# Local attention on one core: projections as three float32r products of high and low parts in place of one fp32 product

## What is computed

```python
def local_attn(x, Wqkv, Wout):          # x is the layer norm with scale ln_w and shift ln_b
    qkv = x @ Wqkv.T                    # (b, 512, 128) @ (128, 1536)
    q, k, v = jnp.split(qkv, 3, axis=-1)
    q, k, v = map(towin, (q, k, v))     # 8 windows of 64 rows, 8 heads of 64
    ke, ve = (expand(k), expand(v))     # each window with its two neighbours
    sim = jnp.einsum('bhnid,bhnjd->bhnij', q, ke) * SCALE
    attn = jax.nn.softmax(jnp.where(valid, sim, -1e9), axis=-1)
    o = jnp.einsum('bhnij,bhnjd->bhnid', attn, ve)
    return o @ Wout.T
```

## Time and profile before

| | |
|---|---|
| median of 3 runs | 1968.98 us (1967.86 to 1974.41) |
| profiled execution, span | 1969.3 us |
| TensorE products busy | 1812.7 us, 92% |
| TensorE weight loads busy | 1293.1 us, 66% |
| VectorE busy | 1463.0 us, 74% |
| ScalarE busy | 1463.6 us, 74% |
| GpSimd busy | 548.0 us, 28% |
| granted TensorE clock, mean | 0.973 |
| projections to queries and keys (L817), each light stage, in pj alone | x244, 132.4 us |
| projections to values (L820), first and second light stage | x128, 69.2 us; x122, 66.4 us |

### The profile page before, as it was taken

The page is one execution under the profiler, slowest core; times in us unless marked ns, Lnnn a source line. Parts: engine busy times, 40 slices in busy tenths (PEclk is TensorE's granted clock), DMA queues, the critical chain, the costliest instruction groups (busy, mean ns, idle before and its releaser), DMA issues. The chain is left out here.

```text
span 1969.3 us, 67306 instructions
## 1 busy us (share of the span) xinstructions
PE 1812.7 (92%) x27305; PEld 1293.1 (66%) x27305; DVE 1463.0 (74%) x3594; ACT 1463.6 (74%) x4168; POOL 548.0 (28%) x668
## 2 busy tenths in 40 slices
PE   3889889888999999999979978899999999997998
PEld 1444444444677777777768865567777777776886
DVE  8999999995676777778865656656777777786553
ACT  4999999984888888887735547588888888773553
POOL 1000000001344444444431107334444444443110
PEclk7999999998999999999989979999999999998998
DMA  6555555530000000000010000010101010002001
GB/s 196 145 141 141 156 142 142 142 77 12 13 19 19 18 19 19 19 23 15 24 46 1 2 1 1 1 23 13 24 13 24 14 24 15 23 19 51 28 28 33
DMA packets 77917, 91.88 MB, mean 47 GB/s; under 512 B 11485, under 2 KB 67650, under 8 KB 77090
## 3 DMA queue, kind: packets, MB, share of 16 engines
q1 hardware_dynamic: 76314, 87.15, 17.5%
q10 hardware_dynamic: 1296, 0.44, 0.1%
HBM read 39.67 MB, written 31.10 MB: 36 GB/s over the span
## 5 line engine op out<-in xcount | busy, mean ns | idle before, releaser
L1419 POOL TENSOR_TENSOR f1l_pn<-f1l_p,f1l_rs 128x512 f32<-128x512 f32 (+1 forms) x256 | 207.9, 833 | 326.0 <-DVE f1l_rs L1140 325.1
L1419 POOL TENSOR_TENSOR f2l_pn<-f2l_p,f2l_rs 128x512 f32<-128x512 f32 (+1 forms) x256 | 207.9, 834 | 297.5 <-DVE f2l_rs L1140 297.4
L1021 ACT ACTIVATE f2l_p<-f2l_sm,f2l_nb 128x192 f32<-128x192 f32 x512 | 212.0, 434 | 44.4 <-DVE f2l_nb L1133 44.4
L1021 ACT ACTIVATE f1l_p<-f1l_sm,f1l_nb 128x192 f32<-128x192 f32 x512 | 211.8, 432 | 42.4 <-DVE f1l_nb L1133 42.4
L513 ACT ACTIVATE r_pr<-r_far 128x1536 f32<-128x1536 f32 x128 | 195.4, 1527 | 3.4 <-PE r_far L387 3.1
L403 PE MATMUL r_acc<-r_pr,r_vp 128*32 128x128 f32 (+2 forms) x3584 | 191.4, 330 | 5.0 <-DVE r_pr L616 3.7
L608 DVE SCALAR_TENSOR_TENSOR r_pr<-r_pr,k_lo,r_cap 128x512 f32<-128x512 f32 x256 | 179.7, 743 | 7.0 <-ACT r_pr L513 6.8
L616 DVE TENSOR_SCALAR r_pr<-r_pr,k_hi,k_lo 128x768 f32<-128x768 f32 x256 | 161.7, 674 | 0.0
L513 ACT ACTIVATE r_pr<-r_near 128x1024 f32<-128x1024 f32 x128 | 139.7, 1091 | 1.5 <-PE r_near L374 1.4
L817 PE MATMUL f1l_pj<-f1l_xt,k_wqkv 128*128 128x512 f32 x244 | 132.4, 624 | 2.6 <-ACT f1l_kt L1003 1.4
L817 PE MATMUL f2l_pj<-f2l_xt,k_wqkv 128*128 128x512 f32 x244 | 132.4, 624 | 2.2 <-ACT f2l_kt L1003 1.4
(11 more groups left out here) (440 smaller groups left out, 4876.8 us busy)
## 6 DMA issues: line engine op xcount, KB each, us to landing
rbf_rows<-r_part SPq DMA_DIRECT2D x112, 128.0 KB, 2.2
r_qs<-rbf_rows SPq DMA_DIRECT2D x60, 192.0 KB
r_ks<-rbf_rows SPq DMA_DIRECT2D x60, 192.0 KB
f1l_vs<-f1l_vv SPq DMA_DIRECT2D x64, 128.0 KB, 2.4
f2l_vs<-f2l_vv SPq DMA_DIRECT2D x64, 128.0 KB, 2.4
rbf_rows<-r_part SPq DMA_DIRECT2D x16, 384.0 KB, 3.0
rbf_rows<-r_part SPq DMA_DIRECT2D x16, 256.0 KB, 3.1
out<-k_x SPq DMA_DIRECT2D x16, 256.0 KB, 2.3
```

The costliest lines, as they stand in the source:

```text
L1021: ins = nc.scalar.activation(p[:, u % 2, k, :], sm[:, u % 2, k // 2, k % 2 * PW:(k % 2 + 1) * PW], ACT.Exp, bias=nb[:, u % 2, k:k + 1], ac ...
L1419: ins = nc.gpsimd.tensor_tensor(pn[:, u % 2, at:at + HU * w].rearrange("p (k c) -> p k c", k=HU), p[:, u % 2, :, cols], r.broadcast_to([P, ...
```

## The change

Both operands of the projections are kept as two float32r parts: high is the value rounded to float32r, low is the rest, rounded in turn. One projection is three products that add up in one bank: low weights by high rows, high by high, high weights by low rows (for values the other way round).

- Weights: wqkv is no longer one load. In the first stage SyncE loads it in thirds to the tile `whole` after batches 1, 2 and 3, and GpSimd writes `wqkv_h` and `wqkv_l`, one copy and one subtraction for each third.
- Rows: xt becomes `xh` and `xl`, two buffers each. GpSimd makes them (`split`, a copy and a subtraction over 128 x 512), for batch 0 VectorE does (`split_first`).
- The transposes of z are no longer k = 0 of `use` but `turn_x`, with semaphores of their own (s_xp, s_xe), and stand at i = TURN_AT = NT - 2 = 2 in the lists of TensorE, ScalarE and GpSimd. They wait for s_pt of unit 2t + 1, the copy of tp by VectorE. In VectorE's list `late` is unchanged (`t % NT == NT - 1`).
- Memory: tiles of the first stage alone are freed after it, yt shares memory with qt, and `one` is a single column that is broadcast.

The core of the diff (new line numbers where a reader needs them are those of the rows of order below):

```diff
@@ stage_rbf, SyncE
             for b in range(B):
                 batch(b, b % 2)
+                if 0 <= b - SPLIT_AT < 3:
+                    q = b - SPLIT_AT
+                    wait(sp, s_wh, 2 * q)
+                    sp.dma_start(whole[:], A["wqkv"][:, THIRD * q:THIRD * (q + 1)]).then_inc(s_wl, 16)
@@ stage_rbf, GpSimd
+            for q in range(3):
+                w = slice(THIRD * q, THIRD * (q + 1))
+                pool.wait_ge(s_wl, 16 * (q + 1))
+                nc.gpsimd.tensor_copy(K["wqkv_h"][:, w], whole[:]).then_inc(s_wh, 1)
+                pool.wait_ge(s_wh, 2 * q + 1)
+                nc.gpsimd.tensor_tensor(K["wqkv_l"][:, w], whole[:], K["wqkv_h"][:, w], ALU.subtract).then_inc(s_wh, 1)
@@ stage_light
-        USES = 1 + 2 * HP + NT
+        USES = 2 * HP + NT
+        TURN_AT = NT - 2
@@ TensorE
-                    mm = nc.tensor.matmul(at, K["wqkv"][:, c * P:(c + 1) * P], xt[:], start=True, stop=True)
+                    w = slice(c * P, (c + 1) * P)
+                    nc.tensor.matmul(at, w_l[:, w], xh[:, par, :], start=True, stop=False)
+                    nc.tensor.matmul(at, w_h[:, w], xh[:, par, :], start=False, stop=False)
+                    if k == 1:
+                        pe.wait_ge(s_xs, 2 * b + 2)
+                    mm = nc.tensor.matmul(at, w_h[:, w], xl[:, par, :], start=False, stop=True)
...
-                    mm = nc.tensor.matmul(at, xt[:, j * P:(j + 1) * P], K["wqkv"][:, 2 * H * DH:3 * H * DH],
-                                          start=True, stop=True)
+                    rows, w = slice(j * P, (j + 1) * P), slice(2 * H * DH, 3 * H * DH)
+                    nc.tensor.matmul(at, xl[:, par, rows], w_h[:, w], start=True, stop=False)
+                    nc.tensor.matmul(at, xh[:, par, rows], w_l[:, w], start=False, stop=False)
+                    mm = nc.tensor.matmul(at, xh[:, par, rows], w_h[:, w], start=False, stop=True)
+
+            def turn_x(b):
+                if b == 1:
+                    pe.wait_ge(s_pe, 2 * HP + (0 if C else 1))
+                elif b > 1:
+                    pe.wait_ge(s_pt, UNITS * (b - 2) + 2 * TURN_AT + 2)
+                pe.wait_ge(s_z, b + 1)
+                at = bank(b, 0)
+                for j in range(NT):
+                    mm = nc.tensor.transpose(at[:, j * P:(j + 1) * P], z[:, j, :], K["ident"][:])
+                mm.then_inc(s_xp, 1)
@@ TensorE, step
-                ahead = i == NT - 1 and b + 2 < B
+                ahead = i == TURN_AT and b + 2 < B
...
                 if ahead:
                     output(t - 1, (2, 3))
-                    use(b + 2, 0)
+                    turn_x(b + 2)
@@ ScalarE, step
-                if i == NT - 1 and b + 2 < B:
-                    leave(b + 2, 0)
+                if i == TURN_AT and b + 2 < B:
+                    leave_x(b + 2)
@@ VectorE
+            def split_first():
+                dve.wait_ge(s_xe, 1)
+                nc.vector.tensor_copy(xh[:, 0, :], xt[:]).then_inc(s_xs, 1)
+                dve.wait_ge(s_xs, 1)
+                nc.vector.tensor_tensor(xl[:, 0, :], xt[:], xh[:, 0, :], ALU.subtract).then_inc(s_xs, 1)
@@ GpSimd
+            def split(b):
+                par = b % 2
+                pool.wait_ge(s_xe, b + 1)
+                wait(pool, s_pp, USES * (b - 1))
+                nc.gpsimd.tensor_copy(xh[:, par, :], xt[:]).then_inc(s_xs, 1)
+                pool.wait_ge(s_xs, 2 * b + 1)
+                nc.gpsimd.tensor_tensor(xl[:, par, :], xt[:], xh[:, par, :], ALU.subtract).then_inc(s_xs, 1)
...
             for t in range(T):
                 if t + 1 < T:
                     normalise(2 * t + 2)
                     normalise(2 * t + 3)
+                if t % NT == TURN_AT and t // NT + 2 < B:
+                    split(t // NT + 2)
                 if t % NT == 1 and t // NT + 2 < B:
                     scaled(t // NT + 2)
```

More of the change, by code:

```diff
@@ L910, in output @@
                     mm.then_inc(s_w, 1)
-            for k in range(1 + 2 * HP):
+            turn_x(0)
+            for k in range(1, 1 + 2 * HP):
                 use(0, k)
@@ L942, in _ @@
                         scores(3)
[L943 removed]
+                turn_x(1)
             else:
[L945 removed]
+                for k in range(1 + 2 * HP, USES + 1):
                     use(0, k)
[L947 removed]
+                turn_x(1)
                 scores(2)
@@ L1327, in _ @@
                 link(nc.vector.reciprocal(K["r2"][:], two[:, 0, :]))
-                for b in range(1, 9):
+                rows(1)
+                split_first()
+                for b in range(2, 9):
                     rows(b)
@@ L2157, in program @@
         K["rtz"] = sb("rtz", [P, 2 * B * (B - 1) + P])
-        for n in ("lo", "hi"):
-            K[n] = sb(n, [P, RH])
-        stage_rbf(nc, K, A)
+        for n in ("wqkv_h", "wqkv_l"):
+            K[n] = sb(n, [P, 3 * H * DH], F32R)
+        K["later"], loads = loads, []
+        load("ident", A["c_ident"], [P, P])
+        with ExitStack() as early:
+            own = lambda n, s, d=F32: early.enter_context(nc.sbuf_tensor("k_" + n, s, d))
+            for n in ("norm_sel", "later_key"):
+                load(n, A["c_" + n], [P, A["c_" + n].shape[1]], own)
+            for n in ("wq", "wk", "wv", "wo"):
+                load(n, A[n], [P, E], own)
+            load("gam", A["gam"].partition_broadcast(P), [P, RH], own)
+            load("gam_p", A["gam_p"], [P, 1], own)
+            for n in ("lo", "hi"):
+                K[n] = own(n, [P, RH])
+            K["first"] = loads
+            stage_rbf(nc, K, A)
         C = {n: sb("c_" + n, [P, 1]) for n in ("dt", "mag", "th", "n", "sin", "cos", "t", "lr", "li", "den",
```

81 lines of the change are left out of this document (41 added, 40 removed).

## The result

The changed kernel ran in 2006.23 us (median of 4 runs, 2004.73 to 2007.87), beside 1969.03 for the kernel before in the same session (4 runs, 1967.86 to 1974.41): a ratio of 1.0189, 95% interval 1.0173 to 1.0205. It is 37 us slower, where 17 were forecast (1986.5, range 1950 to 2028). The profiled execution has a span of 2005.3 us.

The account below looks back on a forecast made before the run. The prediction took a loop over ScalarE, TensorE and VectorE to bound the light stages. Its terms, 16.2 - 3.4 + 4.4 = +17.2 us on the kernel before, gave 1986.5 us, range 1950 to 2028.

Parts of the forecast that it names:

- ordinary batches: Light stages: gains in the steps and the stall from moved transposes sum to 0.58 longer a batch, 28 batches, +16.2 us.
- batch 14, twice: Batch 14 of each light stage: no transposes moved, only the projection gain stays, 4 x 0.42 = 1.7, twice: -3.4 us.
- start of the two stages: First rows' splits uncovered, about +2.4 us; first batch's 12 projections give back 12 x 0.21: 0, +-1.5 a stage.
- weight splits: First stage: six GpSimd operations slow VectorE by 0 to 0.73 us each; upper end taken, +4.4 us.
- the loop over three engines: Light-stage step: chain through ScalarE, TensorE and VectorE from one first exponential (E) to the next, 7.85 us before the change.
- the stall: At i = 2 TensorE idles 1.5 us before the moved transposes, as VectorE takes the residual before its copies; E 9.81 apart.
- the cover of GpSimd's splits: Light stage: GpSimd's row splits end about E + 10.2, needed only a step later; cost nothing, uncovered up to 2 x 1.04 a batch.
- Rival 1: Light stage: the loop has unseen slack and TensorE's own work decides; about 1952 us, faster; chance 22%.
- 2 (weights exposed): Projections: each f32r product's weights load only after the product before, 0.97 a projection, no gain; 2029 us; chance 10%.
- 3 (two passes): Projections: an f32r record streams two passes, 1.39 a projection, TensorE bounds all steps; about 2190 us; chance 4%.
- 4 (stall hidden): Step i = 2: the stall is hidden and all of 2.56 us a batch is gained; 1891 us; chance 3%.
- the price of a projection: TensorE: three one-pass f32r products take 0.64 us with the first load covered, 0.75 without; 0.21 less than before.

Follow-up runs that it names:

- the halves: Changed kernel with the second and third f32r product of each projection cut into two pieces of 256 columns: 2010.41 us, ratio 1.02.

## Why the prediction was right in kind and wrong in size

| step | forecast | measured |
|---|---|---|
| ordinary batches | 28 x 0.58 = 16.2 | 28 x 0.94 = 26.3 |
| the search's batches | 0 | 6 to 8 |
| batch 14, twice | -3.4 | -0.8 |
| last residual of each stage | 0 | 1.9 |
| start of the two stages | 0 | -0.3 and +1.2 |
| weight splits | 4.4 | 4.8 |
| sum | 17.2 | 39 to 41; time +37.2 |

The start is counted to the first residual, in the first stage from the last row statistics (58.7 us before, 58.4 after), in the second from TensorE's first transposes (29.3 and 30.5). The rows come from several profiles, and the work between the end of the first light stage and the start of the second, which the change does not touch, took 261.9 and 257.5 us in the two profiles of the kernel before: the sum can't be expected to meet the time closer than this.

**Right**: the loop over three engines as the bound, the stall and where it comes from (1.5 us forecast, 1.31 measured on TensorE; 0.7 and 0.61 before the values at i = 3), the single pass of f32r, the cover of GpSimd's splits. Rival 1 (TensorE's work decides) falls with the distances of E and with the runs with four products and with fp32, 2 (weights exposed) with the starts 0.23 apart and the halves, 3 (two passes) with the same starts, 4 (stall hidden) with the 1.31. The weight splits' price was partly luck: it took the upper end of 0 to 0.73 us, from operations of 1.04; measured are 0.80 for operations of 1.2 on average.

**The step that failed** is the price of a projection, "3 x 0.213 = 0.64 with its first load covered, 0.75 without". It takes 0.80, for 0.96. The assumption on the loads, "I let the three loads cost no more than one does", held: the first product holds the engine 0.34, which is 0.11 more than the others, and the 0.75 has that in it. But a product is 0.23, not 0.213. Instead of 0.21 a projection saves 0.16. Seven projections a batch lie in the chain (the prediction counted six; a fourth product costs 1.65 a batch, seven times 0.23), and 0.05 each is 0.35 of the 0.36 that a batch is over the forecast, 10 us of the 20 missing. Step by step it fits less well: 0.11, 0.10, 0.02 and 0.13 over. At i = 2 the price and the stall, which was 0.2 shorter, nearly cancel; at i = 3 the prediction's own terms add up to 5.31 and not 5.37, and some 0.1 stays open.

**A second term was put at nothing without a reason.** The prediction priced the stall for an ordinary batch and multiplied by 28. In batches 12 and 13 VectorE carries the search, which costs the kernel before only 1.5 us in its first step (9.38 for 7.85, much as after the change, 9.14 for 7.52) and nothing after it (31.93 from residual to residual, as any batch). The stall put VectorE into the chain, so what it does there counts: 0.65 at each of four stalls and some 0.6 a stage in the steps beside them, 3.8 in all, and 1.5 more wherever TensorE's granted clock fell after the longer wait. Together that was 8 in one profile and 6 in the other. In batch 14, where nothing is moved, the search runs on (to step 61), and of the 0.42 a step that the prediction gave to it only 0.16 to 0.25 came: E lie 7.50, 7.69, 7.62 and 7.58 apart, for 7.73, 7.85, 7.87 and 7.75 before. With the search behind the copies all four are 7.83 to 7.85, so its place sets them. From residual to residual, as the batches above are counted, batch 14 is 29.26 for 29.68.

**A third was TensorE's clock at the end of a stage.** In each light stage the last residual comes 0.92 later after the one before it (6.95 for 6.03, both profiles). It waits for the last eight output products, before the change and after it:

```profile
1804.16 1.16 PE L907 MATMUL f2l_xa<-k_wout_l,f2l_ot 128*128 128x128 f32 x8 [0.60 <-DVE f2l_ot L1158]
1803.00:1805.40 2.40, 1.72 (x24) 1.35 (x16) 0.47 (x2) 0.61 (x2) 0.00 (x0) 1.00 0.00 0
...
1839.54 2.08 PE L946 MATMUL f2l_xa<-k_wout_l,f2l_ot 128*128 128x128 f32 x8 [0.60 <-DVE f2l_ot L1202]
1839.50:1842.00 2.50, 2.08 (x8) 1.78 (x8) 0.29 (x1) 0.00 (x0) 0.00 (x0) 0.50 0.00 0
```

They take 2.08 us at a granted clock of 0.50 and 1.16 at 1.00. In both kernels TensorE has pauses of 0.6 to 0.95 us in front of them; before the change the clock falls only after the last residual. The change alone does not decide it: the run with six times the splits, whose light stages are those of the changed kernel, has 6.95 in the first and 6.03 in the second. Why the fall comes earlier in one stage than in another stays open.

## What to carry to other kernels

When an operation moves on one engine, look through the written order of every other engine for the exception that was made for its old place. Here one stale condition turned a gain of 28 us into a loss of 37. A stall is priced not only by its length in an ordinary step: it also lays bare all that the stalled engine has to do there at other times, and in a third of the longest stalls here TensorE came out at half its clock. And a loop that bounds gives back a saving only down to the next loop; here that was 0.25 us a step away.
